# Mask rows spread over more slots, a new order on VectorE behind the encoder's attention, and a layer norm applied on ScalarE for three groups

## The chip, the cores and the metric

One core of one Trainium2 chip runs the whole program in one launch. The metric is device time in microseconds (us), of the slowest core where there are several; here there is one. Five engines with queues of their own take part: TensorE (PE), VectorE (DVE), ScalarE (ACT), GpSimd (POOL) and SyncE (SP), which here only issues DMAs. They wait for one another by semaphores written out by hand.

## The reference

The input x has shape 8 x 512 x 128. Two blocks follow each other, each as x + layernorm(block(layernorm(x))):

```python
# block 1: attention of all 4096 tokens to 512 shared keys, 16 heads of 8
q = relu(x @ Wq.T + bq); k = relu(keys @ Wk.T + bk); v = relu(values @ Wv.T + bv)
a = softmax(q k.T / sqrt(8)) v            # per head
out1 = transpose(a).reshape(x.shape) + x
# block 2: an encoder layer. Attention runs over the 8 batch rows, 4 heads of 32
y1 = ln1(x + mha(x))                      # "the norm behind the encoder's attention"
# top-1 routing to 8 experts with a capacity of 512 tokens; linear experts
gates = softmax(y1 @ wg); idx = argmax(gates)
y2 = ln2(y1 + gate * ((y1 @ w1[idx] + b1[idx]) @ w2[idx] + b2[idx], 0 if over capacity))
```

## The kernel before

**First part (to about 377 us).** The first attention is cut into 32 slots (`kappa` 0 to 31): half of the batch rows for two heads each. In a slot, PE computes the scores of 8 items by rows, VectorE takes their maxima out of PSUM (`reduce_rows`, eight per slot), GpSimd splits the maxima into three bf16 parts (`split_max`), PE turns them, ScalarE copies them (`max_turned`), and SP loads them by two DMAs as shift rows into the stack of the next slot (`load_shift`). PE then computes the scores by columns (`score_columns`, L1587), ScalarE takes the exponentials, and PE multiplies with v (`multiply_v`). SP's queue in a slot is, in this order: six DMAs of the stack three slots ahead (`load_stack`, L1294), in every fourth slot two of the keys (`load_keys`, L1299), the two shift rows (L1305), four stores of the attended rows (L1320). In slots 2 to 5, `load_c` (L1314) adds four DMAs each, sixteen in all, which spread the bf16 parts of the experts' combined bias over rows of `c_rows`. GpSimd copies these rows twice into `c_stack` in its slot 6, and writes the mask rows into it by two `affine_select` in slot 7 and two in slot 8 (L1494). The experts at the end need `c_stack`.

While the slots of one group of heads run, GpSimd finishes the group before: `pool_group` with `pool_divide` (the attended rows by their softmax sums), residual and two layer norms. The last group (g = 3) has no slots behind it, so that its part falls into the back end: `pool_divide` on GpSimd, the norms (called LAST1 and LAST2 here) on VectorE. LAST2 makes the encoder's input of group 3, announced by the semaphore `s_n2l`.

**Back end (from about 378 us).** The tokens are in four groups of 1024 (g = 0 to 3, eight tiles of 128 x 128). The encoder's attention takes each group in two halves, q = 0 to 7. The order on each engine is written out. For a half: PE `scores2(q)` (L623, L629), VectorE `compact(q)` (a maximum over PSUM, L944, then two small steps to L949), ScalarE `softmax_exp(q)` (L815), VectorE `normalise(q)` (L954 to L958), GpSimd `spread(q)` (L516, four instructions of 128 x 512), PE `spread_turned(q)` (L660), ScalarE two copies `copy_turned` (L820), PE `attend(q)` (L669), ScalarE `copy_attended(q)` (L826). For a group: PE `turn_tokens` and `project` (L608, L613), ScalarE's copies of them (L791, L797, L802), then PE `project_out(g)` (L677), VectorE `residual(g)` (L965), and the norm ln1: statistics and five small instructions (`norm_smalls`, L259 to L265), ScalarE's square root (`root`, L303), VectorE's `norm_invert` (L269, L271), and `norm_apply`, eight tensor_scalar of 128 x 128 (L280). GpSimd's `affine1(g)` (L527, four instructions) follows, and PE turns the result (`turn_y1`). VectorE then routes the group (`choose(g)`, L983 to L992) and selects among the experts (`select`, L1008), PE computing them tile by tile (L651, L653).

Exponential and square root lie in different tables of ScalarE; between them stands an ACT_TABLE_LOAD. A load stands right in front of its instruction and doesn't wait for what the instruction waits for.

Of the kernel before, what the change touches and what calls it, by code (L numbers as in the profile page):

```python
# [5 lines left out]
D = 128  # L6
B = 8
S = 512
G = S // P
NH, DH = 16, 8  # L10
NH2, HD2 = 4, 32
E, FF = 8, 512
E2 = E // 2
# [3 lines left out]
QB = 4  # L17
# [5 lines left out]
PARTS = 3  # L23
# [8 lines left out]
QPG = 2  # L32
# [20 lines left out]
def build(nc, x, keys, values, wq, bq, wk, bk, wv, bv, win, bin_, wout, bout,  # L53
# [8 lines left out]
    with ExitStack() as ctx:  # L62
# [3 lines left out]
        def sem(name):  # L66
            return ctx.enter_context(nc.semaphore(name))
# [9 lines left out]
        X = sb("X", [P, G, B, D])  # L77
# [34 lines left out]
        def view(space, lo, dims, dt=F32, parts=P):  # L112
# [6 lines left out]
            if len(dims) == 1:  # L119
# [99 lines left out]
             "logits_ready", "logits_copied", "expert_masks_ready", "gate_exp_done", "tokens_counted", "weights_ready"))  # L219
        (s_xp, s_sel, s_wa, s_i4, s_n4, s_i5, s_n5, s_y2, s_y2l, s_am, s_aq, s_asd, s_af1, s_sum2, s_out) = (sem(n) for n in  # L220
            ("experts_done", "expert_selected", "weighed_by_act", "norm4_scale_ready",
             "norm4_done", "norm5_scale_ready", "norm5_done", "output_ready", "last_output_ready", "act_means", "act_squares", "act_deviation_ready", "second_affine_done", "third_sum_ready", "output_stored"))
# [8 lines left out]
        def norm_variance(dve, ch, src, st6, small):  # L231

            for b in range(B):
                ins = dve.bn_stats(st6[:, b, :], src(b))  # L234
            ch.done(ins)
            ch.wait()
            norm_smalls(dve, ch, st6, small)

# [50 lines left out]
        def tiles(t, g):  # L289
            return lambda b: t[:, g, b, :]  # L290
# [115 lines left out]
        def pool_divide(pool, ch, g):  # L406

            pool.wait_ge(s_al, 64 * (g + 1))
            pool.wait_ge(s_rb, 64 * (g + 1))
            ch.done(pool.tensor_tensor(A[:, g], A[:, g], INV, MUL))  # L410
            ch.wait()
            pool.tensor_tensor(A[:, g], A[:, g], XN[:, g], ADD).then_inc(s_r1, 1)

# [373 lines left out]
        def back_end_act(act):  # L787
# [35 lines left out]
            def copy_attended(q):  # L823
# [4 lines left out]
                               ACT.Identity, bias=bias_col[:, 5:6]).then_inc(s_ot, 1)  # L828

            copy_tokens(1)  # L830
            softmax_exp(0)
# [15 lines left out]
            copy_attended(2)  # L847
            root(act, LAST2, smallo)
            copy_turned(3, 0, 4)
            copy_turned(3, 1, 6)  # L850
            softmax_exp(4)
            copy_attended(3)
            copy_y1(0, 6)
# [5 lines left out]
            copy_turned(4, 1, 6)  # L859
            copy_attended(4)  # L860
            softmax_exp(6)
            copy_logits(0)
# [8 lines left out]
            root(act, LN1[2])  # L871
            copy_attended(6)
            copy_logits(1)
            copy_turned(7, 0, 4)
# [65 lines left out]
        def back_end_dve(dve, ch):  # L940
# [27 lines left out]
            def variance1(g):  # L968
                dve.wait_ge(s_res, g + 1)
                norm_variance(dve, ch, tiles(A, g), st6, small)  # L970

            def apply1(g):
                norm_invert(dve, ch, LN1[g], small)
                norm_apply(dve, tiles(A, g), tiles(A, g), small).then_inc(s_n3, 1)

# [36 lines left out]
            compact(0)  # L1012
            normalise(0)
            dve_invert(dve, last)
            for q in range(1, 2 * QPG):
                compact(q)
                normalise(q)
            residual(0)
            dve.wait_ge(s_r1, G)
            norm_variance(dve, ch, tiles(A, last), st6o, smallo)  # L1020
            variance1(0)
            norm_invert(dve, ch, LAST1, smallo)
# [4 lines left out]
            ch.wait()  # L1027
            norm_variance(dve, ch, tiles(X, last), st6o, smallo)
            compact(4)
            norm_invert(dve, ch, LAST2, smallo)  # L1030
            norm_apply(dve, tiles(X, last), tiles(A, last), smallo).then_inc(s_n2l, 1)
            normalise(4)
            compact(5)
# [22 lines left out]
            residual(g)  # L1056
            dve.wait_ge(s_res, G)
            norm_variance(dve, ch, tiles(A, g), st6, small)
            select(5)
# [192 lines left out]
        def _(sp):  # L1252
# [54 lines left out]

            def load_c(k):

                sp.wait_ge(s_csplit, 1)  # L1310
                sp.wait_ge(s_cz, 1)
                c_k = c_rows[32 * k:32 * k + PARTS, :].rearrange("q (r j d) -> q r j d", r=2, d=D)
                for j in range(E2):
                    sp.dma_start(c_k[:, :, j, :], c_parts[32 * j:32 * j + 1]).then_inc(s_cl, 16)  # L1314
# [54 lines left out]
            def slot(kappa):  # L1369
# [12 lines left out]
                if kappa:  # L1382
                    sp.wait_ge(s_pve, kappa)
                    store_attended(kappa - 1)

            for kappa in range(NQ):
                g, c = kappa // 8, kappa % 8
                slot(kappa)
                if c == 1 and g:
                    load_denominators(g - 1)  # L1390
                if c == 2 and g:
                    load_attended(g - 1)
                    store_inverses(g - 1)
# [13 lines left out]
        def _(pool):  # L1407
# [61 lines left out]
            def build(kappa):  # L1469

                if kappa == 1:
                    pool.wait_ge(s_qp, B)
                    pool.memset(c_rows, 0.0).then_inc(s_cz, 1)
                if kappa == 5:
                    pool.wait_ge(s_wu, E)
                    pool.memset(others, 0.0).then_inc(s_oz, 1)
                if kappa == 2:
                    pool.wait_ge(s_const, 6)
                    for h in range(NH2):
                        ch.done(pool.affine_select(out=own_row[:], in_=own_row[:], compare_op=ALU.not_equal, fill=1.0,  # L1480
                                                   base=-HD2 * h, pattern=[[0, B], [-1, 16]], channel_multiplier=1))
                        ch.wait()
                    pool.tensor_scalar(other_row[:], own_row[:], -1.0, BIG, ADD, MUL).then_inc(s_rm, 1)
                if kappa == 6:
                    pool.wait_ge(s_cl, 16 * E2 * QB)
                    for v in range(2):
                        ch.done(pool.tensor_copy(c_stack[:, v, :].rearrange("p (d e) -> p e d", e=E),
                                                 c_rows.rearrange("p (e d) -> p e d", d=D)))
                    ch.wait()
                if kappa in (7, 8):  # L1490
                    c_v = c_stack[:].rearrange("p v (d e) -> p v d e", e=E)
                    for k in (2 * (kappa - 7), 2 * (kappa - 7) + 1):
                        pool.wait_ge(s_cb, k)
                        pool.affine_select(out=c_v, in_=c_v, compare_op=ALU.not_equal, fill=-BIG, base=-32 * k - MASK_ROW,  # L1494
                                           pattern=[[-E, 2], [0, D], [-1, E]], channel_multiplier=1).then_inc(s_cb, 1)
# [426 lines left out]
```

## Time and profile before

| | us |
|---|---|
| runs | 583.43, 583.67, 587.01: median 583.67 |
| the profiled execution | 585.64, of which the span of instructions 583.9 |
| busy: PE / DVE / ACT / POOL | 491.2 / 509.8 / 410.3 / 224.8 |
| mean granted TensorE clock | 0.946 of full speed |

All times below are those of the profiled execution, counted from the start of its span. In a timeline row stand start, duration, engine, line, operation, the written and read tiles with partitions x elements, how many instructions were merged, and in square brackets how long the engine had been idle before and what released it. The program's names are those of buffers: `space` stands for views of several large ones. A row merged from several instructions gives the time from the start of the first to the end of the last.

### The profile page before, as it was taken

To read this page: it belongs to the slowest core of one execution; us is meant where nothing else is said; L and a number is where in the kernel's file an instruction comes from. 1 tells how busy PE (TensorE), PEld (TensorE's weight loads), DVE (VectorE), ACT (ScalarE), POOL (GpSimd) and SP (SyncE) were. 2 spreads that over 40 slices of the span, in tenths; PEclk is the share of its full clock that TensorE was granted. 3 is DMA by queue.
4 is the path that set the end of the run, shared out by engine and by line. 5 is a ranking of instruction groups with operands and counts; after the bars stand their busy time and mean duration, and the time that the engine had idled before them with its cause. 6 is when DMAs were issued, how large, how long until landed. Compare 5 with 4: busy or idle time off the path is not lost.

```text
span 583.9 us, 10824 instructions
## 1 busy us (share of the span) xinstructions
PE 491.2 (84%) x3955; PEld 202.6 (35%) x3955; DVE 509.8 (87%) x821; ACT 410.3 (70%) x837; POOL 224.8 (38%) x345
## 2 busy tenths in 40 slices
PE   1887799989999999999999999887578898987900
PEld 1545122222222222222222222365457564433300
DVE  4979899969999999999999995369988759899986
ACT  1743499969999999999999998644446321144963
POOL 8000212029801766726676344868366330000000
PEclk9979599979999999999999999999988999999965
DMA  9945011111113111132111310020000000000112
GB/s 237 299 152 146 28 29 33 29 31 34 33 42 100 44 35 31 43 91 57 33 28 41 79 50 13 11 83 1 1 2 1 1 1 0 2 0 0 36 36 72
DMA packets 31796, 28.99 MB, mean 50 GB/s; under 512 B 6256, under 2 KB 23800, under 8 KB 31744
## 3 DMA queue, kind: packets, MB, share of 16 engines
q1 hardware_dynamic: 29712, 27.33, 16.8%
q10 hardware_dynamic: 2032, 0.98, 0.7%
q8 instruction: 31, 0.51, 0.4%
q14 instruction: 21, 0.17, 0.1%
HBM read 19.23 MB, written 8.65 MB: 48 GB/s over the span
## 4 chain that ended last, share of the span: by engine, by line
PE 48%; DVE 40%; ACT 7%; issue 3%; DMA 1%; SPq 0%; DVEq 0%; ACTq 0%
PE ps L1598 16%; DVE row_max L1845 16%; PE ps L1587 9%; PE ps L1560 8%; DVE space L1008 4%; PE ps L653 2%; DVE space L944 2%; ACT space L1767 2%; ACT space L897 2%; DVE st L234 1%; PE ps L608 1%; PE ps L660 1%; PE ps L343 1%; DVE space L280 1%; DVE XN L280 1%
## 5 line engine op out<-in xcount | busy, mean ns | idle before, releaser
L1845 DVE TENSOR_REDUCE row_max<-ps 128x2 f32<-128x1024 f32 x256 | 293.6, 1218 | 10.8 <-PE ps L1560 8.1
L1767 ACT ACTIVATE space<-ps 128x512 f32<-128x512 f32 x512 | 269.4, 598 | 13.7 <-PE ps L1587 10.5
L1598 PE MATMUL ps<-space 128*32 128x512 f32 (+1 forms) x1504 | 151.6, 475 | 0.4
L1560 PE MATMUL ps<-space 48*128 48x512 bf16 x512 | 132.8, 395 | 12.0 <-DVE row_max L1845 10.1
L1587 PE MATMUL ps<-space 51*128 51x512 bf16 x512 | 135.2, 388 | 1.9 <-DMA space<-max_turned 1.9
L1438 POOL CAST max_parts<-row_max 128x16 bf16<-128x16 f32 x32 | 6.3, 196 | 186.8 <-DVE row_max L1845 186.8
L1587 PEld LDWEIGHTS ps<-space 51*128 51x128 bf16 x512 | 41.2, 94 | 73.4 <-ACT space L1767 51.1
L653 PE MATMUL ps<-W,space 128*128 128x512 f32 x128 | 65.4, 592 | 0.0
L1560 PEld LDWEIGHTS ps<-space 48*128 48x128 bf16 x512 | 26.3, 94 | 72.9 <-DVE row_max L1845 37.4
L1598 PEld LDWEIGHTS ps<-space 128*32 128x32 f32 x1504 | 29.8, 108 | 62.7 <-issue 35.5
L1008 DVE TENSOR_REDUCE space<-ps 128x128 f32<-128x1024 f32 x32 | 38.6, 1218 | 9.0 <-PE ps L653 8.8
L516 POOL TENSOR_TENSOR space<-PC,same_row 128x512 f32<-128x512 f32 x32 | 33.0, 1062 | 18.9 <-DVE PC L958 11.0
L651 PE MATMUL ps<-c_stack,w1T 128*128 128x512 bf16 x64 | 24.4, 381 | 9.3 <-DVE space L1008 9.3
L653 PEld LDWEIGHTS ps<-W,space 128*128 128x128 f32 x128 | 24.4, 191 | 16.1 <-issue 14.4
L944 DVE TENSOR_REDUCE space<-ps 128x128 f32<-128x2048 f32 x8 | 18.2, 2278 | 6.6 <-PE ps L629 6.6
L527 POOL TENSOR_TENSOR space<-space,rows 128x512 f32<-128x512 f32 x12 | 15.0, 1268 | 18.9 <-DVE space L280 18.7
L303 ACT ACT_TABLE_LOAD x5 | 6.4, 1283 | 22.0 <-DVE small L265 22.0
L820 ACT COPY space<-ps 128x1024 f32<-128x1024 f32 x16 | 15.6, 1012 | 8.9 <-PE ps L660 8.9
L660 PE MATMUL ps<-ident,space 128*128 128x128 f32 x128 | 16.3, 281 | 5.0 <-issue 3.0
L1774 ACT COPY attended<-ps 128x512 f32<-128x512 f32 x32 | 18.7, 586 | 2.0 <-PE ps L1598 2.0
L425 POOL TENSOR_TENSOR XN<-XN 128x256 f32<-128x256 f32 (+4 forms) x40 | 15.8, 394 | 3.1
L660 PEld LDWEIGHTS ps<-ident,space 128*128 128x128 f32 x128 | 14.3, 143 | 7.0 <-issue 4.1
(245 smaller groups left out, 648.8 us busy)
## 6 DMA issues: line engine op xcount, KB each, us to landing
space<-q_parts_dram SPq DMA_DIRECT2D x64, 48.0 KB
attended_dram<-attended SPq DMA_DIRECT2D x128, 18.0 KB
X<-in_L_attn_queries SPq DMA_DIRECT2D x8, 256.0 KB, 7.5
space<-in_L_ffn_w SPq DMA_DIRECT2D x2, 1024.0 KB, 6.0
space<-q_parts_dram SPq DMA_DIRECT2D x64, 32.0 KB
space<-attended_dram SPq DMA_DIRECT2D x16, 128.0 KB, 2.9
space<-inverses_dram SPq DMA_DIRECT2D x16, 128.0 KB
out<-space SPq DMA_DIRECT2D x4, 512.0 KB, 3.2
```

The lines of the kernel that those rows point to most:

```text
L516: pool.tensor_tensor(EX[:, half, 4 * h:4 * h + 4, :].rearrange("p t (m n) -> p t m n", n=16), PC[:, q, 4 * h:4 * h + 4, :].rearrange("p t ...
L651: pe.matmul(ps[:, bank + half, :], others[:, g, b // 2, :], c_stack[:, b % 2, cols], start=True, stop=False)
L653: mm = pe.matmul(ps[:, bank + half, :], YT[:, g, b, :], W[:].rearrange("p d e -> p (d e)")[:, cols], start=False, stop=True)
L660: mm = pe.transpose(ps[:, bank + k // 4, (k % 4) * P:(k % 4 + 1) * P], EX[:, q % QPG, 8 * pair + k, :], ident[:])
L944: dve.tensor_reduce(SC[:, q].rearrange("p a m -> p (a m)"), ps[:, 0:4, :].rearrange("p a (t n) -> p (a t) n", n=16), AX.X, MAX).then_inc(s ...
L1008: dve.tensor_reduce(YT[:, k // B, k % B, :], ps[:, bank:bank + 2, :].rearrange("p a (d e) -> p (a d) e", e=E), AX.X, MAX).then_inc(s_sel, 1)
L1560: mm = pe.matmul(ring(n)[:, a, :], q_stack[rows_a, kappa % 4, item * P:item * P + P], k_rows[rows_a, kappa // 4 % 2, :], start=True, stop= ...
L1587: pe.matmul(ps[:, col_bank(v), :], k_rows[rows_a, kappa // 4 % 2, tc * P:(tc + 1) * P], q_stack[rows_a, kappa % 4, b * S:(b + 1) * S], sta ...
L1598: mm = pe.matmul(ps[32 * m:32 * m + 32, PV, cols], v_heads[:, tc, PAIR * (kappa // 4) + m % PAIR, :], probs[(TC * kappa + tc) % 3][:, m, c ...
L1767: act.activation(probs[(TC * kappa + tc) % 3][:, m, :], ps[:, col_bank(v), :], ACT.Exp, scale=1.0 / math.sqrt(DH)).then_inc(s_pr, 1)
L1774: act.copy(attended[:, kappa % 2, :], ps[:, PV, :]).then_inc(s_pve, 1)
L1845: dve.tensor_reduce(row_max[:, par].rearrange("p (a c) -> p a c", a=PAIR)[:, :, item], ring(n), AX.X, MAX).then_inc(s_free, 1)
```

## The change

`load_c` issues three DMAs in each of slots 2, 3, 4, 6, 7 and one in slot 8, where it issued four in each of slots 2 to 5. GpSimd's two copies into `c_stack` move from slot 6 to slots 9 and 10 (one each), its two pairs of mask rows from slots 7 and 8 to slots 11 and 19. The last group's `pool_divide` works on four pieces of two tiles.

In the back end VectorE takes `compact(1)` ahead of the last group's reciprocal, both statistics of LAST1 and ln1 of group 0 ahead of their small steps, and `compact(4)` and `normalise(4)` ahead of LAST2's inverse and apply. For groups 0 to 2 `norm_apply` of ln1 leaves VectorE: it announces the scale (`s_i1`), and ScalarE applies it by eight activations in a new `apply1(g)`, which stands behind `copy_attended` of half 2, 4 and 6. ScalarE's root for LAST2 moves behind `softmax_exp(4)`.

```diff
         def pool_divide(pool, ch, g):
...
-            ch.done(pool.tensor_tensor(A[:, g], A[:, g], INV, MUL))
-            ch.wait()
-            pool.tensor_tensor(A[:, g], A[:, g], XN[:, g], ADD).then_inc(s_r1, 1)
+            parts = [slice(0, B)] if g < G - 1 else [slice(lo, lo + 2) for lo in range(0, B, 2)]
+            for part in parts:
+                ch.done(pool.tensor_tensor(A[:, g, part], A[:, g, part], INV[:, part], MUL))
+            ch.wait()
+            for part in parts:
+                ins = pool.tensor_tensor(A[:, g, part], A[:, g, part], XN[:, g, part], ADD)
+            ins.then_inc(s_r1, 1)
...
+            def apply1(g):
+                act.wait_ge(s_i1, g + 1)
+                for b in range(B):
+                    ins = act.activation(A[:, g, b, :], A[:, g, b, :], ACT.Identity, scale=small[:, 3, b:b + 1],
+                                         bias=small[:, 4, b:b + 1])
+                ins.then_inc(s_n3, 1)
...
             copy_attended(2)
-            root(act, LAST2, smallo)
+            apply1(0)
             copy_turned(3, 0, 4)
             copy_turned(3, 1, 6)
             softmax_exp(4)
+            root(act, LAST2, smallo)
             copy_attended(3)
...
             copy_attended(4)
+            apply1(1)
             softmax_exp(6)
             copy_logits(0)
...
             copy_attended(6)
+            apply1(2)
             copy_logits(1)
...
             def variance1(g):
                 dve.wait_ge(s_res, g + 1)
+                dve.wait_ge(s_n3, g)
                 norm_variance(dve, ch, tiles(A, g), st6, small)
 
             def apply1(g):
-                norm_invert(dve, ch, LN1[g], small)
-                norm_apply(dve, tiles(A, g), tiles(A, g), small).then_inc(s_n3, 1)
+                norm_invert(dve, ch, LN1[g], small, s_i1)
...
             compact(0)
             normalise(0)
+            compact(1)
             dve_invert(dve, last)
-            for q in range(1, 2 * QPG):
+            normalise(1)
+            for q in range(2, 2 * QPG):
                 compact(q)
                 normalise(q)
             residual(0)
             dve.wait_ge(s_r1, G)
-            norm_variance(dve, ch, tiles(A, last), st6o, smallo)
-            variance1(0)
+            dve.wait_ge(s_res, 1)
+            norm_statistics(dve, tiles(A, last), st6o)
+            ch.done(norm_statistics(dve, tiles(A, 0), st6))
+            ch.wait()
+            norm_smalls(dve, ch, st6o, smallo)
+            norm_smalls(dve, ch, st6, small)
             norm_invert(dve, ch, LAST1, smallo)
             ch.done(norm_apply(dve, tiles(A, last), tiles(A, last), smallo))
             ch.wait()
             ch.done(dve.tensor_tensor(X[:, last], X[:, last], A[:, last], ADD))
             apply1(0)
             ch.wait()
-            norm_variance(dve, ch, tiles(X, last), st6o, smallo)
+            ch.done(norm_statistics(dve, tiles(X, last), st6o))
             compact(4)
+            ch.wait()
+            norm_smalls(dve, ch, st6o, smallo)
+            normalise(4)
             norm_invert(dve, ch, LAST2, smallo)
             norm_apply(dve, tiles(X, last), tiles(A, last), smallo).then_inc(s_n2l, 1)
-            normalise(4)
             compact(5)
             residual(1)
             normalise(5)
...
-            def load_c(k):
+            def load_c(lo, hi):
...
-                for j in range(E2):
+                for i in range(lo, hi):
+                    k, j = i // E2, i % E2
...
                     sp.dma_start(c_k[:, :, j, :], c_parts[32 * j:32 * j + 1]).then_inc(s_cl, 16)
...
+            C_SLOTS = (2, 3, 4, 6, 7, 8)
...
-                if 2 <= kappa < 2 + QB:
-                    load_c(kappa - 2)
+                if kappa in C_SLOTS:
+                    first = 3 * C_SLOTS.index(kappa)
+                    load_c(first, min(first + 3, E2 * QB))
...
-                if kappa == 6:
+                if kappa in (9, 10):
+                    v = kappa - 9
                     pool.wait_ge(s_cl, 16 * E2 * QB)
-                    for v in range(2):
-                        ch.done(pool.tensor_copy(c_stack[:, v, :].rearrange("p (d e) -> p e d", e=E),
-                                                 c_rows.rearrange("p (e d) -> p e d", d=D)))
+                    ch.done(pool.tensor_copy(c_stack[:, v, :].rearrange("p (d e) -> p e d", e=E),
+                                             c_rows.rearrange("p (e d) -> p e d", d=D)))
                     ch.wait()
-                if kappa in (7, 8):
+                if kappa in (11, 19):
                     c_v = c_stack[:].rearrange("p v (d e) -> p v d e", e=E)
-                    for k in (2 * (kappa - 7), 2 * (kappa - 7) + 1):
+                    for k in (0, 1) if kappa == 11 else (2, 3):
```

The last group's own ln1 stays on VectorE and only gains a wait for the third `apply1`.

## Rows read from the trace of the kernel before

**Rows 1.** Timeline of VectorE, slots 5 and 6 and those around them.

```profile
127.96 1.23 DVE L1845 TENSOR_REDUCE row_max<-ps 128x2 f32<-128x1024 f32 x1 [2.88 <-PE ps L1560]
130.86 2.44 DVE L1845 TENSOR_REDUCE row_max<-ps 128x2 f32<-128x1024 f32 x2 [1.68 <-PE ps L1560]
133.79 41.69 DVE L1845 TENSOR_REDUCE row_max<-ps 128x2 f32<-128x1024 f32 x36 [0.49 <-PE ps L1560]
```

**Rows 2.** Timeline of SP's DMA queue, slots 2, 5 and 7.

```profile
94.45 2.98 SPq L1314 DMA_DIRECT2D space<-c_parts  x4
...
121.38 1.55 SPq L1299 DMA_DIRECT2D space<-k_rows_dram  x2
122.97 1.51 SPq L1305 DMA_DIRECT2D space<-max_turned  x2
...
137.75 3.78 SPq L1294 DMA_DIRECT2D space<-q_parts_dram  x6
142.88 1.49 SPq L1305 DMA_DIRECT2D space<-max_turned  x2
144.42 1.51 SPq L1320 DMA_DIRECT2D attended_dram<-attended  x4
```

**Rows 3.** Timeline of PE in slot 5.

```profile
124.96 0.39 PE L1587 MATMUL ps<-space 51*128 51x512 bf16 x1 [1.49 <-DMA space<-max_turned]
```

**Rows 4.** Timeline of POOL, slot 7.

```profile
141.81 7.75 POOL L1494 TENSOR_SCALAR_AFFINE_SELECT c_stack<-c_stack 128x2048 bf16<-128x2048 bf16 x2
```

**Rows 5.** Timeline of ScalarE around the places of the new applies.

```profile
416.35 0.69 ACT L826 ACTIVATE space<-ps,bias_col 128x512 f32<-128x512 f32 x1 [1.22 <-PE ps L669]
422.10 0.30 ACT L303 ACTIVATE smallo<-smallo,eps 128x8 f32<-128x8 f32 x1 [5.07 <-DVE smallo L265]
...
424.23 1.28 ACT L815 ACT_TABLE_LOAD   x1
...
445.20 0.69 ACT L826 ACTIVATE space<-ps,bias_col 128x512 f32<-128x512 f32 x1 [1.22 <-PE ps L669]
...
447.81 0.31 ACT L815 ACTIVATE PC<-space 128x128 f32<-128x128 f32 x1 [0.62 <-DVE space L949]
448.02 0.19 ACT L811 COPY logits<-ps 128x64 f32<-128x64 f32 x1
```

**Rows 6.** The chain that ended last: an apply by ScalarE in a later norm.

```profile
534.69 3.19 ACT space L897 x8
```

**Rows 7.** Timeline of VectorE in the back end.

```profile
404.76 1.64 DVE L234 BATCH_NORM_STATS2 st6o<-space 128x6 f32<-128x128 f32 x8
...
425.27 2.14 DVE L280 TENSOR_SCALAR space<-X,smallo 128x128 f32<-128x128 f32 x8
...
433.06 1.23 DVE L965 TENSOR_TENSOR space<-ps,XN 128x1024 f32<-128x1024 f32 x1 [1.47 <-PE ps L677]
...
444.20 2.29 DVE L944 TENSOR_REDUCE space<-ps 128x128 f32<-128x2048 f32 x1 [1.73 <-PE ps L629]
...
450.35 0.95 DVE L987 TENSOR_SCALAR space<-space 128x64 f32<-128x64 f32 x1
...
473.19 0.20 DVE L987 TENSOR_SCALAR space<-space 128x64 f32<-128x64 f32 x1
...
478.64 1.23 DVE L1008 TENSOR_REDUCE space<-ps 128x128 f32<-128x1024 f32 x1 [2.10 <-PE ps L653]
```

**Rows 8.** Timeline of POOL in the back end.

```profile
416.99 5.05 POOL L527 TENSOR_TENSOR space<-space,rows 128x512 f32<-128x512 f32 x4 [9.08 <-DVE space L280]
...
449.18 4.10 POOL L516 TENSOR_TENSOR space<-PC,same_row 128x512 f32<-128x512 f32 x4 [1.56 <-issue]
```

**Rows 9.** Timeline of PE in the back end.

```profile
424.33 0.61 PE L623 MATMUL ps<-other_row,own_row 32*128 32x512 bf16 x4 [5.27 <-DVE space L944]
...
435.06 3.70 PE L608 MATMUL ps<-space,wT 128*128 128x512 f32 x8 [1.16 <-ACT space L791]
```

**Rows 10.** Busy time by stretch (PE, PEld, DVE, ACT, POOL), granted PE clock, DMA share, GB/s.

```profile
424.00:431.00 7.00, 5.51 (x77) 4.48 (x77) 6.72 (x19) 3.57 (x6) 2.65 (x3) 0.64 0.00 0
```

More of the change, by code:

```diff
@@ L219, in build @@
              "logits_ready", "logits_copied", "expert_masks_ready", "gate_exp_done", "tokens_counted", "weights_ready"))
-        (s_xp, s_sel, s_wa, s_i4, s_n4, s_i5, s_n5, s_y2, s_y2l, s_am, s_aq, s_asd, s_af1, s_sum2, s_out) = (sem(n) for n in
-            ("experts_done", "expert_selected", "weighed_by_act", "norm4_scale_ready",
+        (s_xp, s_sel, s_wa, s_i1, s_i4, s_n4, s_i5, s_n5, s_y2, s_y2l, s_am, s_aq, s_asd, s_af1, s_sum2, s_out) = (sem(n) for n in
+            ("experts_done", "expert_selected", "weighed_by_act", "norm1_scale_ready", "norm4_scale_ready",
              "norm4_done", "norm5_scale_ready", "norm5_done", "output_ready", "last_output_ready", "act_means", "act_squares", "act_deviation_ready", "second_affine_done", "third_sum_ready", "output_stored"))
@@ L231, in norm_variance, with norm_statistics @@
         def norm_variance(dve, ch, src, st6, small):
+            ch.done(norm_statistics(dve, src, st6))
+            ch.wait()
+            norm_smalls(dve, ch, st6, small)
+        def norm_statistics(dve, src, st6):
             for b in range(B):
                 ins = dve.bn_stats(st6[:, b, :], src(b))
-            ch.done(ins)
-            ch.wait()
-            norm_smalls(dve, ch, st6, small)
+            return ins
         def st64(g):
@@ L1019, in back_end_dve @@
             dve.wait_ge(s_r1, G)
-            norm_variance(dve, ch, tiles(A, last), st6o, smallo)
-            variance1(0)
+            dve.wait_ge(s_res, 1)
[3 more added lines that the diff above has]
+            norm_smalls(dve, ch, st6o, smallo)
+            norm_smalls(dve, ch, st6, small)
             norm_invert(dve, ch, LAST1, smallo)
@@ L1057, in back_end_dve @@
             dve.wait_ge(s_res, G)
+            dve.wait_ge(s_n3, g)
             norm_variance(dve, ch, tiles(A, g), st6, small)
@@ L1306, in load_shift @@
                                  max_turned[turned, kappa % 2, :]).then_inc(s_shift[a], 16)
-            def load_c(k):
+            def load_c(lo, hi):
                 sp.wait_ge(s_csplit, 1)
                 sp.wait_ge(s_cz, 1)
-                c_k = c_rows[32 * k:32 * k + PARTS, :].rearrange("q (r j d) -> q r j d", r=2, d=D)
-                for j in range(E2):
+                for i in range(lo, hi):
+                    k, j = i // E2, i % E2
+                    c_k = c_rows[32 * k:32 * k + PARTS, :].rearrange("q (r j d) -> q r j d", r=2, d=D)
                     sp.dma_start(c_k[:, :, j, :], c_parts[32 * j:32 * j + 1]).then_inc(s_cl, 16)
```

## The prediction

> **What bounds the kernel now.** I read the page first: PE and VectorE are both busy for some 85% of the span, so the mean tells nothing, and each stage has to be read by itself. I took the timeline of VectorE for the first part. A slot is eight maxima over PSUM, and they run back to back: 36 in 41.69 us, 1.158 each, so a slot takes 9.26 us [rows 1]. That is VectorE's pace, and only in slots 5 and 6 does it break: idle times of 2.88, 1.68 and 0.49 us, 5.05 in all, put down to PE. PE in its turn waited there 1.49 us for the shift rows [rows 3], which SP issued late. So SP's queue binds two slots of the first part.
>
> In the back end I read the timelines of all five engines beside each other, since every step of a half waits for the one before it on another engine. Two places bear on the change. ScalarE stands 5.07 us at LAST2's root [rows 5], holding up the copies behind it, and PE then resumes after 5.27 us of idle time [rows 9]. And behind `copy_attended(4)` ScalarE has 0.62 us to spare after its table load before `softmax_exp(6)` [rows 5]: VectorE, GpSimd and PE all go on from that exponential.
>
> **Mask rows.** In a plain slot SP's issues take 3.78 + 1.49 + 1.51 = 6.78 us of 9.26 [rows 2]; 2.48 are free. Four DMAs of `load_c` take 2.98 and don't fit: three slots in a row fall behind, and in slot 5 the keys' 1.55 come on top. Three DMAs take 2.24 and fit. What remains is slot 5: the keys stand ahead of the shift, and the stack starts late behind slot 4's three. On time the shift would be at 142.88 - 2 x 9.26 - 5.05 = 119.3. Of the 2.48 free us 142.88 - 137.75 - 3.78 = 1.35 lie between stack and shift and 1.13 ahead of the stack; 2.24 of `load_c` make the stack 1.1 late and leave 0.2 ahead of the shift, and the keys add 1.55, so it goes out near 120.7. PE would have taken it without waiting if issued by 122.97 - 1.49 = 121.5. That leaves 0.8 us. I take the whole 5.05 as gained; the lower bound is half of it, if slot 5 still stalls. SP isn't late in slot 9, since slot 8 gets one DMA only. GpSimd's mask rows take 7.75 us for two [rows 4]; with that in slot 7 VectorE ran its 36 maxima without a gap [rows 1], so slots 11 and 19, where no group work stands, hold it as well. The copies, one to a slot, are shorter. `c_stack` isn't needed before the experts. All this costs nothing while GpSimd's slot lasts under 9.26; without that cover it would cost the excess.
>
> **The reorder up to group 0.** LAST1's small steps now stand behind eight more statistics, 1.64 us [rows 7], and ScalarE's copies of group 2's projections queue behind LAST1's root. Against this VectorE comes earlier to that place, since `compact(1)` no longer waits behind the reciprocal and the waits for exponentials are filled; I estimate 0 to 2.3 us. So `copy_attended(2)`, which ends at 416.35 + 0.69 = 417.04 [rows 5], moves by +1.6 to -0.7; I take +0.5, 417.5. `pool_divide` in four pieces has the same elements and six more instructions; it starts later, because the reciprocal does, but is wanted only behind `residual(0)`. I price it at 0 (bounds 0 and +0.5: GpSimd's next `spread` is put off).
>
> **Apply on ScalarE, group 0.** Eight activations of this shape took 3.19 us in a later norm [rows 6]. From 417.5 ScalarE does apply 3.19, two copies 424.23 - 422.40 = 1.83, table 1.28, exponential 0.31, table 1.28, root 0.30 [rows 5]: 425.7. Two table loads are new, because exponential and root of LAST2 have changed places. VectorE has `compact(4)` done long before and waits. GpSimd's `affine1(0)`, 5.05 us [rows 8], now runs from 420.7 to 425.8, and `normalise(4)`, a product of two SBUF operands, ends with it. The inverse takes 0.4, and LAST2's apply can start at 426.4 instead of 425.27.
>
> Here is the step I am least sure of. `normalise(4)` now goes first and releases `spread(2,0)`, so the apply's eight tensor_scalar run beside four GpSimd instructions, 4.10 us. No row shows these eight beside a GpSimd tensor_tensor. The nearest: a tensor_scalar of `choose(0)` took 0.95 us beside `spread`, and 0.20 without [rows 7, 8]. The bounds are 2.14 (no hindrance), so 428.5 for `s_n2l`, and one instruction let through per GpSimd instruction: 426.05 + 4.10, then five of 0.27, 431.5. It was 427.4. I take 431.5, by the nearer row.
>
> From there VectorE does `compact(5)` (444.20 to 447.81 for its like, of which some 0.65 was hindrance: 2.95) and `residual(1)` 1.2; PE follows 0.25 later: `project(3)` at 435.9, against 435.06 [rows 9], +0.85. Before, VectorE waited 1.47 us for PE ahead of that residual [rows 7]; this wait is gone, and what is late is VectorE itself.
>
> **Apply on ScalarE, groups 1 and 2.** VectorE saves 2.14 each, but behind group 1 it waited 1.73 us for PE anyway [rows 7]: worth nothing. ScalarE pays: `copy_attended(4)` ended at 445.89; with +1.0 (the 0.85, and small steps of group 1 a little more hindered) 446.9. Then apply 3.19, table 1.28, exponential 0.31: 451.7, against 448.12 [rows 5], +3.6. Behind it are queued `copy_logits(0)`, for which PE waits, and VectorE's `normalise(6)`, `choose(0)` and `compact(7)`, which was busy without a break before. These meet `affine1(1)` (1.26 per instruction) where they met `spread` (1.03): +0.4. For group 2 the logits come 2 us later and `choose(1)` runs beside `affine1(2)`: up to 4 x 0.75 = 3.0, of which 2.10 vanish in VectorE's wait ahead of a select [rows 7]; +0.6 (bounds 0 and +1.0). From there on VectorE runs nearly without a gap, so the rest moves along.
>
> **Sum.** -5.05 + 1.0 + 2.6 + 0.4 + 0.6 = -0.45 us. The profiled execution would be 585.64 - 0.45 = 585.2; it lies 1.97 above the median of the runs, so against the median 583.67 I predict 583.2.
>
> **Rivals.**
> *The apply isn't hindered.* `s_n2l` comes at 428.5, `project(3)` at 432.9, 2.15 early; `softmax_exp(6)` is still 0.55 late, since apply and table load stand in front of it. Back end +1.55, net -3.5: 580.2. Against it stands the 0.95 row; for it, that those instructions waited for each other by semaphores and these eight don't. On this the Trainium skill, "SBUF — State Buffer", section "Who interferes with whom", says that the pair of ports that VectorE and GpSimd share is an exclusive lock which the first to start holds for its whole instruction. By that rule, VectorE getting in first would block GpSimd instead, and the time would be this rival's; the 0.95 row shows GpSimd first.
> *Slower: TensorE's clock.* In the forecast PE idles some 3 us ahead of `project(3)`, where it idled 1.16. After 5.27 us of idle time the stretch behind had a granted clock of 0.64, a mixture of 1.2 and 2.4 GHz [rows 9, 10]. If `project(3)` (3.70 us) falls to the lower level, the first half of it takes 1.85 more, and the rest some 0.5 that ScalarE's root doesn't hide: net +1.9, 585.6. It decides as soon as the granted clock in that stretch is below 1.
> *The mask rows don't do what they should.* Slot 5 still stalls: half gained gives 585.7, nothing gained 588.3. The 0.8 us of room speak against it.
> *All goes well:* the reorder gains its 0.7, nothing hinders, and group 2 costs nothing: 578.4 or less.
>
> **How the numbers follow.** Forecast 0.44, apply not hindered 0.24, clock 0.15, mask rows 0.10, better than all that 0.07. The range 578.5 to 587.0 leaves out the last and the worst parts of the second and third rival, some 0.15. A change under 1% (5.8 us) can hardly be told from none in this kernel, by the spread of the three runs. Under 577.8 lies most of the best case and a little of errors I don't see: 0.10; over 589.5 0.05; 0.85 between.
>
> **What would show it.** VectorE's idle times of slots 5 and 6 are gone, and the slots' maxima follow each other at 9.26 us; SP's shift of slot 5 goes out behind the keys without PE waiting. ScalarE shows five more microseconds between `copy_attended(2)` and LAST2's root, two more table loads, and `softmax_exp(6)` directly behind one. LAST2's eight tensor_scalar take about 5 us together, or 2.14 if the first rival holds. The prediction is wrong if the applies start at other times than given (a wait for `s_i1` on ScalarE would do it), or if VectorE has idle time behind group 3's residual that takes the delay back.

## The result, and the profile after

The changed kernel is slower: 589.91 us (median of 13 runs, 586.38 to 592.62) against 584.08 us for the kernel before beside it (13 runs, 581.80 to 587.38); ratio 1.0088, 95% interval 1.0067 to 1.011. The prediction was 583.2, range 578.5 to 587.0, with 0.85 on a change of less than 1%: the ratio lies within that 1%, the time outside the range. The profiled execution took 588.79 us with a span of 587.1, 3.2 above the span of before. That is less than the 5.1 us of the ratio, because before's profiled execution lies 1.6 us above the median of its kernel and that of the changed kernel 1.1 below; the traces hold only part of the difference.

**The first part did what the forecast said.** The timeline of VectorE in the changed kernel (start, duration, engine, line, operation, count, idle time before), which answers to [rows 1]:

```profile
72.65 97.25 DVE L1875 TENSOR_REDUCE row_max<-ps 128x2 f32<-128x1024 f32 x84 [1.71 <-PE ps L1590]
```

84 maxima in 97.25 us without a gap, 1.158 each: the three idle times of before are gone. SP's queue around slot 5, which answers to [rows 2]:

```profile
112.71 2.25 SPq L1342 DMA_DIRECT2D space<-c_parts  x3
115.01 3.78 SPq L1321 DMA_DIRECT2D space<-q_parts_dram  x6
118.83 0.77 SPq L1326 DMA_DIRECT2D space<-k_rows_dram  x2
119.65 1.51 SPq L1332 DMA_DIRECT2D space<-max_turned  x2
```

The shift of slot 5 went out at 119.65, against 120.7 forecast and 121.5 needed, mostly because the keys took 0.77 us here and not 1.55. The back end's `compact(0)` starts at 374.85 instead of 380.20: 5.35 us gained.

**The back end gave it all back, and 3.2 us more.** So I counted its steps from the start of `compact(0)` in either trace:

| step, us since `compact(0)` | before | after | moved | forecast |
|---|---|---|---|---|
| LAST1's root, ScalarE | 28.17 | 29.77 | +1.6 | |
| `copy_attended(2)` | 36.15 | 38.88 | +2.7 | +0.5 |
| LAST2's root | 41.90 | 47.37 | +5.5 | +3.3 |
| end of LAST2's apply (`s_n2l`) | 47.21 | 53.52 | +6.3 | +4.1 |
| `project(3)` | 54.86 | 57.73 | +2.9 | +0.85 |
| `softmax_exp(6)` | 67.61 | 73.50 | +5.9 | +3.6 |
| `compact(7)` | 73.09 | 79.36 | +6.3 | +4.0 |
| `residual(2)` | 79.46 | 87.36 | +7.9 | +4.0 |
| `residual(3)` | 100.58 | 109.04 | +8.5 | +4.6 |
| end of the span | 203.70 | 212.25 | +8.55 | +4.6 |

The forecast errs in two steps: 2.2 us by `copy_attended(2)`, and 1.6 between `compact(7)` and `residual(2)`. Everything between keeps its distance from the forecast.

*The first step* begins behind LAST1's statistics. VectorE's timeline of the changed kernel there (before: [rows 7]):

```profile
399.94 1.63 DVE L240 BATCH_NORM_STATS2 st<-space 128x6 f32<-128x128 f32 x8
401.60 0.55 DVE L263 TENSOR_TENSOR smallo<-st6o 128x8 f32<-128x8 f32 x1
402.07 1.09 DVE L264 TENSOR_TENSOR smallo<-st6o 128x8 f32<-128x8 f32 x1
403.09 1.09 DVE L265 TENSOR_TENSOR smallo<-st6o 128x8 f32<-128x8 f32 x1
404.21 0.17 DVE L267 SCALAR_TENSOR_TENSOR smallo<-smallo 128x8 f32<-128x8 f32 x1
```

GpSimd's timeline beside it:

```profile
390.24 2.84 POOL L416 TENSOR_TENSOR space<-space 128x256 f32<-128x256 f32 x4 [2.05 <-DMA space<-inverses_dram]
393.15 2.82 POOL L419 TENSOR_TENSOR space<-space,XN 128x256 f32<-128x256 f32 x4
395.94 8.21 POOL L524 TENSOR_TENSOR space<-PC,same_row 128x512 f32<-128x512 f32 x8
```

And GpSimd's timeline of the kernel before, with the same divide and the later of the two `spread`:

```profile
394.17 2.37 POOL L410 TENSOR_TENSOR space<-space 128x1024 f32<-128x1024 f32 x1
396.61 2.35 POOL L412 TENSOR_TENSOR space<-space,XN 128x1024 f32<-128x1024 f32 x1
...
403.79 4.13 POOL L516 TENSOR_TENSOR space<-PC,same_row 128x512 f32<-128x512 f32 x4 [0.44 <-DVE PC L958]
```

The divide waits 2.05 us for the inverses, since the reciprocal comes later now, and in its four pieces it takes 5.73 us (390.24 to 395.97) where it took 4.79. So two `spread` run back to back until 404.15; counted from `compact(0)` that is 1.6 later than before. LAST1's small steps on tiles of 128 x 8, 0.17 us each when alone (404.21), take up to 1.09 beside them. Before, too, they began beside `spread`, but it ended 1.5 us after they started (407.92); now it ends 2.6 after. The root is 1.6 late, of which 0.5 are the eight statistics moved ahead, less what VectorE gained, as forecast, and 1.1 the small steps. As an estimate from these rows, the divide in one piece would have let `spread` end 0.9 earlier; no run tried it. PE then has stood idle for 3.75 us (1.07 before), and the 32 matmuls of projection V and `spread_turned` take 2.53 and 3.13 us where they took 2.05 and 1.95; 1.1 of that reaches `copy_attended(2)`.

*The second step* is `project_out(2)`. PE's timeline of the kernel before, at the projection V, at `spread_turned` and at `project_out(2)`:

```profile
409.73 2.05 PE L613 MATMUL ps<-wT,space 128*128 128x128 f32 x16 [1.07 <-ACT space L797]
412.10 1.95 PE L660 MATMUL ps<-ident,space 128*128 128x128 f32 x16 [0.32 <-issue]
...
457.57 2.05 PE L677 MATMUL ps<-wT,space 128*128 128x128 f32 x16 [2.44 <-ACT space L807]
```

PE's timeline of the changed kernel, from the first step on (the rows of `project(3)` and ahead of it answer to [rows 9]):

```profile
405.97 2.53 PE L621 MATMUL ps<-wT,space 128*128 128x128 f32 x16 [3.75 <-ACT space L805]
408.30 3.13 PE L668 MATMUL ps<-ident,space 128*128 128x128 f32 x16
...
425.81 3.78 PE L685 MATMUL ps<-wT,space 128*128 128x128 f32 x16 [1.16 <-ACT space L815]
...
432.58 3.70 PE L616 MATMUL ps<-space,wT 128*128 128x512 f32 x8 [1.28 <-ACT space L799]
...
458.49 3.68 PE L685 MATMUL ps<-wT,space 128*128 128x128 f32 x16 [3.02 <-ACT space L815]
```

The windows of the changed kernel (length, busy time of PE, PEld, DVE, ACT and POOL with counts, granted clock, DMA share, GB/s; [rows 10] is the third of before):

```profile
404.00:419.00 15.00, 10.87 (x152) 9.92 (x152) 10.03 (x37) 10.81 (x18) 1.58 (x3) 0.89 0.01 1
419.00:424.00 5.00, 2.40 (x38) 2.14 (x39) 2.94 (x5) 4.04 (x6) 4.64 (x5) 0.70 0.00 0
424.00:431.00 7.00, 5.84 (x28) 5.33 (x26) 6.91 (x11) 2.36 (x3) 5.39 (x4) 0.50 0.00 0
...
445.00:454.00 9.00, 5.23 (x77) 4.87 (x80) 5.32 (x9) 5.75 (x11) 6.81 (x6) 0.81 0.00 0
454.00:462.00 8.00, 4.98 (x41) 4.54 (x34) 4.69 (x11) 1.96 (x4) 5.75 (x7) 0.79 0.00 0
```

`project_out(2)`, 16 matmuls, takes 3.68 us after 3.02 idle; before, it took 2.05. VectorE waits for it with `residual(2)`: the 1.6 us. `project_out(1)` ran wholly at the lower level (granted 0.50 in its window), `project(3)` at the upper one (granted 0.99 from 431 to 445).

*As forecast* are the steps of ScalarE from `copy_attended(2)` to LAST2's root. Its timeline in the changed kernel, which answers to [rows 5]:

```profile
413.73 0.69 ACT L834 ACTIVATE space<-ps,bias_col 128x512 f32<-128x512 f32 x1 [1.25 <-PE ps L677]
414.31 3.18 ACT L841 ACTIVATE space<-space,small 128x128 f32<-128x128 f32 x8
417.39 1.90 ACT L828 COPY space<-ps 128x1024 f32<-128x1024 f32 x2
419.31 1.28 ACT L823 ACT_TABLE_LOAD   x1
420.60 0.31 ACT L823 ACTIVATE PC<-space 128x128 f32<-128x128 f32 x1
420.93 1.28 ACT L307 ACT_TABLE_LOAD   x1
422.22 0.30 ACT L307 ACTIVATE smallo<-smallo,eps 128x8 f32<-128x8 f32 x1
```

So is LAST2's apply. VectorE's timeline, which answers to [rows 7], and then GpSimd's beside it ([rows 8]):

```profile
424.02 4.35 DVE L284 TENSOR_SCALAR space<-X,smallo 128x128 f32<-128x128 f32 x8
```

```profile
422.90 4.11 POOL L524 TENSOR_TENSOR space<-PC,same_row 128x512 f32<-128x512 f32 x4 [0.28 <-issue]
```

The apply has `spread` beside it until 427.01. After that 1.36 us remain, which is five instructions at 0.27 (2.14 / 8); so three got through in 2.99 us, about one per GpSimd instruction of 1.03.

### The profile page after: what moved, and what is told of

Its sections match the earlier page's. It is cut to its first block, busy times and chain, and to the rows that moved or that the text cites. A ratio compares the mean times of both kernels' runs of the same rounds, so it can differ in the third digit from the quotient of the medians.

```text
span 587.1 us, 10839 instructions
## 1 busy us (share of the span) xinstructions
PE 492.0 (84%) x3955; PEld 207.2 (35%) x3955; DVE 505.8 (86%) x797; ACT 421.6 (72%) x863; POOL 225.8 (38%) x351
## 4 chain that ended last, share of the span: by engine, by line
PE 48%; DVE 39%; ACT 7%; issue 2%; DMA 1%; ACTq 1%; DVEq 0%
DVE row_max L1875 18%; PE ps L1628 16%; PE ps L1617 9%; PE ps L1590 8%; DVE space L1026 4%; PE ps L661 2%; ACT space L915 2%; PE ps L668 2%; DVE space L962 2%; DMA w_in<-in_L_ffn_out_proj_w 1%; PE ps L616 1%; DVE space L284 1%; PE ps L347 1%; ACT space L841 1%; PE ps L621 1%
## 5 line engine op out<-in xcount | busy, mean ns | idle before, releaser
L1628 PE MATMUL ps<-space 128*32 128x512 f32 (+1 forms) x1504 | 150.0, 471 | 0.4
L1617 PE MATMUL ps<-space 51*128 51x512 bf16 x512 | 133.6, 384 | 0.0
L668 PE MATMUL ps<-ident,space 128*128 128x128 f32 x128 | 18.6, 304 | 6.9 <-issue 4.7
L668 PEld LDWEIGHTS ps<-ident,space 128*128 128x128 f32 x128 | 16.7, 160 | 9.0 <-issue 5.7
```

Source lines behind the costliest of these rows:

```text
L668: mm = pe.transpose(ps[:, bank + k // 4, (k % 4) * P:(k % 4 + 1) * P], EX[:, q % QPG, 8 * pair + k, :], ident[:])
L1617: pe.matmul(ps[:, col_bank(v), :], k_rows[rows_a, kappa // 4 % 2, tc * P:(tc + 1) * P], q_stack[rows_a, kappa % 4, b * S:(b + 1) * S], sta ...
L1628: mm = pe.matmul(ps[32 * m:32 * m + 32, PV, cols], v_heads[:, tc, PAIR * (kappa // 4) + m % PAIR, :], probs[(TC * kappa + tc) % 3][:, m, c ...
```

## The experiments

A profile's first part differs from execution to execution: `compact(0)` started at 372.86 to 376.07 in ten kernels with the new mask rows. So beside each ratio (to the kernel before, run beside it on the same chip) the table gives the back end of the profiled execution, from `compact(0)` to the end of the span.

| kernel | median us | ratio, 95% interval | back end us |
|---|---|---|---|
| before | 584.1 to 585.5 | 1 | 203.7 |
| changed | 589.91 | 1.0088 [1.0067, 1.011] | 212.25 |
| mask_rows_only | 580.07 | 0.9912 [0.988, 0.9943] | 204.6 |
| back_end_only | 594.27 | 1.0149 [1.0119, 1.018] | 212.45 |
| reciprocal_early | 587.90 | 1.0045 [1.0026, 1.0063] | 211.3 |
| applies_on_vector | 584.46 | 0.9986 [0.9963, 1.0009] | 207.3 |
| group1_on_vector | 587.44 | 1.0037 [1.001, 1.0064] | 210.8 |
| apply_before_normalise | 588.67 | 1.0074 [1.0043, 1.0104] | 211.9 |
| changed_pe_filled | 587.28 | 1.0037 [1.0017, 1.0056] | 210.6 |
| mask_rows_compact4 | 579.61 | 0.9916 [0.9886, 0.9947] | 203.0 |
| mask_rows_filled | 583.99 | 0.9978 [0.9961, 0.9995] | 205.5 |
| compact4_filled | 581.02 | 0.9929 [0.9909, 0.9948] | 203.9 |

**The two halves of the change, each alone.** `mask_rows_only` is the kernel before with this part of the change:

```diff
-                if 2 <= kappa < 2 + QB:
-                    load_c(kappa - 2)
+                if kappa in C_SLOTS:                     # (2, 3, 4, 6, 7, 8)
+                    first = 3 * C_SLOTS.index(kappa)
+                    load_c(first, min(first + 3, E2 * QB))
...
-                if kappa == 6:
+                if kappa in (9, 10):
...
-                if kappa in (7, 8):
+                if kappa in (11, 19):
```

> The kernel before with the mask rows alone spread over more slots (SP's and GpSimd's part of the change). If the first part did what the two traces show, the back end starts 5.3 us earlier and nothing gives it back: ratio to before 0.991, VectorE without idle time in slots 5 and 6. If the rival holds, that an earlier start of the back end costs it time of its own (by the place of its idle times against TensorE's clock), less than 3 us remain: 0.995 or more.

Measured 0.9912, 5.1 us gained. Its maxima on VectorE's timeline run as in the changed kernel:

```profile
71.12 97.28 DVE L1848 TENSOR_REDUCE row_max<-ps 128x2 f32<-128x1024 f32 x84 [1.29 <-PE ps L1563]
```

`back_end_only` is the changed kernel with these lines as before.

> The changed kernel with the mask rows as before. If the loss is the back end's own, it shows in full: 8.5 us between its start and its end as in the two traces, ratio 1.015. If the loss comes from the two parts together, under 1.010.

Measured 1.0149. The halves add up within the noise: 0.9912 x 1.0149 = 1.0060, uncertain by some 0.0044, against 1.0088 for both. The mask rows are worth what was forecast for them; all the rest of the change costs some 8.7 us. The back end of `back_end_only` took as long as that of the changed kernel, but lost its time at other places: there the projection V took 3.78 us after 4.25 of idle time, and `project_out(2)` 2.05 after 2.32. So the 1.6 us at `project_out(2)` are those of the changed kernel's profiled execution; the same order can lose more at the first step and nothing there.

**The late reciprocal.**

```diff
             compact(0)
             normalise(0)
-            compact(1)
             dve_invert(dve, last)
+            compact(1)
             normalise(1)
```

> The changed kernel with the last group's reciprocal ahead of compact(1), where it was. My theory: the late reciprocal makes the inverses land late, GpSimd's division and both spreads of group 1 follow 1.6 us later, and they hinder LAST1's small steps, behind which ScalarE's copies and PE's V projection wait; PE's idle time of 3.75 us there lowers its clock. Then LAST1's root comes 1.5 us earlier, copy_attended(2) 2 to 2.7 us, and the ratio falls from 1.009 to about 1.004. Rival: the eight statistics put ahead of those small steps are the delay; then less than 0.5 us change.

Measured 1.0045, as the number said, but not in the way that the theory said. GpSimd is through with `spread` at 403.35, and LAST1's small steps take 0.17 each. Yet the root comes only 0.56 us earlier counted from `compact(0)`, where 1.5 were expected, because VectorE itself got to the statistics 1.7 later. Of these, 1.0 come from other small steps that had met GpSimd instead (396.07 and 398.06 below; the same two took 0.35 and 0.77 in the changed kernel). VectorE's timeline of `reciprocal_early`:

```profile
396.07 1.00 DVE L967 TENSOR_TENSOR space<-space,mx 128x128 f32<-128x128 f32 x1
...
398.06 1.10 DVE L976 TENSOR_TENSOR PC<-PC,sm 128x128 f32<-128x128 f32 x1
...
403.62 0.17 DVE L263 TENSOR_TENSOR smallo<-st6o 128x8 f32<-128x8 f32 x1
```

PE's timeline of the same run:

```profile
405.75 2.05 PE L621 MATMUL ps<-wT,space 128*128 128x128 f32 x16 [1.64 <-ACT space L805]
...
431.14 5.20 PE L616 MATMUL ps<-space,wT 128*128 128x512 f32 x8 [2.42 <-ACT space L799]
```

What it did win is PE's clock at the projection V (2.05 us after 1.64 idle): `copy_attended(2)` is 1.76 earlier. Further on it lost part of that, by the very event of the slower rival in the prediction: `project(3)` took 5.20 us instead of 3.70. What is left is 0.9 us by the back end and 2.5 by the ratios, uncertain by some 1.7.

**The applies back on VectorE**, all three, and in another kernel group 1's alone.

```diff
# ScalarE
             copy_attended(2)
-            apply1(0)
... the same behind copy_attended(4) and copy_attended(6)
# VectorE, apply1(g), for g = 0 to 2
-                norm_invert(dve, ch, LN1[g], small, s_i1)
+                norm_invert(dve, ch, LN1[g], small)
+                norm_apply(dve, tiles(A, g), tiles(A, g), small).then_inc(s_n3, 1)
```

> The changed kernel with the three applies of ln1 back on VectorE, all else as changed. If the applies on ScalarE are the main loss, groups 0, 1 and 2 give back about 1, 2.5 and 0.6 us and what PE's clock loses behind them (1.6): 5 to 6 us, ratio 0.999. If the order of VectorE is the main loss, less than 2.5 us come back: 1.005 or more.

> The changed kernel with the apply of group 1 alone back on VectorE. By the prediction's step for group 1, softmax_exp(6) comes 2.5 us earlier and compact(7) 2.5 to 2.9: ratio 1.004. If VectorE's own apply (2.14 us) then delays compact(6), less than 1 us: 1.007.

Measured 0.9986 and 1.0037, as the numbers said. So moving the applies cost about 5 us of the back end (212.25 against 207.3), and the rest of the new order, with the divide in pieces and the two new table loads, 2.7 (207.3 against 204.6 for the mask rows alone); by the ratios 6.0 and 4.3. Group 1's apply by itself is worth 1.4 us by the back end, 3.0 by the ratios, uncertain by some 2. Its steps didn't move as expected: counted from `compact(0)`, `softmax_exp(6)` came 0.7 us earlier and `compact(7)` 1.1, not 2.5, for in that execution `project(3)` started 0.9 later and took 5.40 us instead of 3.70. With all three applies back, PE still idled 4.18 us ahead of the projection V, and later 3.06 ahead of `project(3)`, and both ran slow, as PE's timeline of `applies_on_vector` shows:

```profile
405.34 2.95 PE L621 MATMUL ps<-wT,space 128*128 128x128 f32 x16 [4.18 <-ACT space L805]
...
429.24 5.85 PE L616 MATMUL ps<-space,wT 128*128 128x512 f32 x8 [3.06 <-ACT space L799]
```

**LAST2's apply out of `spread`'s way.**

```diff
-            normalise(4)
             norm_invert(dve, ch, LAST2, smallo)
             norm_apply(dve, tiles(X, last), tiles(A, last), smallo).then_inc(s_n2l, 1)
+            normalise(4)
```

> The changed kernel with LAST2's inverse and apply ahead of normalise(4) again, so that no GpSimd spread runs beside the apply. The eight tensor_scalar then take 2.14 us instead of 4.35 and s_n2l comes some 3 us earlier. If that hindrance is on the path (as the prediction has it), project(3) starts 2 us earlier: ratio 1.005. Rival: project_out(1) on a slow PE (3.78 us) and turn_tokens(3) behind it end as late as exp(5), so that at most 0.5 us is won: 1.008.

Measured 1.0074, not to be told from the change. The eight instructions took 2.14 us, with GpSimd idle beside them, and were done 3.0 us earlier counted from `compact(0)`. VectorE's timeline of this run:

```profile
422.78 2.14 DVE L284 TENSOR_SCALAR space<-X,smallo 128x128 f32<-128x128 f32 x8
```

PE made little of it: `project_out(1)` still ran at the lower level, the turns behind it (428.28) came late, and `project(3)` started only 0.8 us earlier, as the rival in the expectation had it. Its timeline:

```profile
424.71 3.79 PE L685 MATMUL ps<-wT,space 128*128 128x128 f32 x16 [1.16 <-ACT space L815]
428.28 1.91 PE L599 MATMUL ps<-ident,space 128*128 128x128 f32 x8
431.36 3.70 PE L616 MATMUL ps<-space,wT 128*128 128x512 f32 x8 [1.16 <-ACT space L799]
```

**TensorE kept busy where it idles.**

```diff
+            def fill(bank, n):
+                for _ in range(n):
+                    pe.matmul(ps[:, bank, :], wT[:, 3, :], W[:].rearrange("p d e -> p (d e)")[:, 0:512], start=True, stop=True)
...
+                if g == 2:                       # ahead of projection V
+                    pe.wait_ge(s_msk, 4)
+                    fill(0, 3)
...                                               # around turn_y1(0): 2 and 1, bank 5
+                    pe.wait_ge(s_msk, 7)         # behind route(0)
+                    fill(0, 3)
...
+                    pe.wait_ge(s_msk, 8)         # ahead of project_out(2)
+                    fill(0, 2)
```

> The changed kernel with extra products on PE whose results nobody reads: 3 of 128 x 512 in the idle time ahead of group 2's V projection, 2 and 1 ahead of turn_y1(0) and project_out(1), 3 behind route(0), 2 ahead of project_out(2). They add work to PE and change nothing else. If the lower TensorE clock behind PE's idle times is what the sum left out, the granted clock stays near 1.0 there, project_out(2) takes 2.05 us instead of 3.7, the V projection and the turns behind it some 1.5 less: 3 us in all, ratio 1.003 to 1.004. If the slow PE is hidden behind other engines, or the added work costs what it saves, 1.008 or more.

Measured 1.0037: some 3 us come back without any of the program's own work being moved (uncertain by 1.7; 1.6 by the back end). The granted clock is 1.00 in three stretches where it was 0.89, 0.81 and 0.79, and `project_out(2)` takes 2.05 us. The windows of this run, then PE's timeline:

```profile
404.00:419.00 15.00, 10.96 (x179) 8.95 (x181) 10.29 (x37) 11.62 (x19) 2.79 (x3) 1.00 0.00 1
...
445.00:454.00 9.00, 6.73 (x90) 4.40 (x89) 5.32 (x9) 6.14 (x11) 7.01 (x7) 1.00 0.00 0
454.00:462.00 8.00, 6.32 (x40) 4.58 (x41) 6.08 (x14) 2.02 (x4) 5.75 (x7) 1.00 0.01 2
```

```profile
406.24 2.05 PE L628 MATMUL ps<-wT,space 128*128 128x128 f32 x16 [1.30 <-ACT space L819]
...
422.21 3.78 PE L611 MATMUL ps<-W,wT 128*128 128x512 f32 x4 [2.73 <-ACT space L848]
...
458.29 2.05 PE L692 MATMUL ps<-wT,space 128*128 128x128 f32 x16
```

The fill at 422.21 (two products, each recorded as two) missed: it came when PE had already idled 2.73 us, ran at the lower level itself, and held up `turn_y1(0)`. What the projection V had won was lost there: `project(3)` starts 58.3 us after `compact(0)`, against 57.7 without the fills.

**A better version?** `mask_rows_only` already beats both kernels. Three more tried to go below it. `mask_rows_compact4` adds to it, without ScalarE's applies, the change's idea of filling the 5 us of ScalarE:

```diff
# ScalarE
-            root(act, LAST2, smallo)
             copy_turned(3, 0, 4)
             copy_turned(3, 1, 6)
+            root(act, LAST2, smallo)
             softmax_exp(4)
# VectorE
-            norm_variance(dve, ch, tiles(X, last), st6o, smallo)
+            ch.done(norm_statistics(dve, tiles(X, last), st6o))
             compact(4)
+            ch.wait()
+            norm_smalls(dve, ch, st6o, smallo)
```

> The kernel before with the mask rows spread, compact(4) ahead of LAST2's small steps, and ScalarE's root for LAST2 behind the two copies of half 3 but ahead of softmax_exp(4) (so no new table loads); the applies stay on VectorE. ScalarE's wait of 5.07 us ahead of those copies should go, PE should turn to attend(3) some 4 us earlier and without 5 us of idle time, and project(3) start 3 to 4 us earlier: ratio 0.985. If VectorE's chain bounds that stretch anyway, 0.990 as with the mask rows alone.

Measured 0.9916, so no gain that the ratios can tell. By the profile `project(3)` came 2.6 us earlier than with the mask rows alone, though `project_out(1)` fell to the lower level (3.58 us); 1.0 was lost next to a `normalise(5)` that now met GpSimd, on VectorE's timeline:

```profile
426.07 1.63 DVE L964 TENSOR_TENSOR PC<-PC,sm 128x128 f32<-128x128 f32 x1
```

(0.66 with the mask rows alone). The back end is 1.6 us shorter in that one execution; the intervals are too wide for it. Then the same products on PE went into both kernels.

> The kernel before with the mask rows spread as in the change, nothing of the back end moved, and products on PE (128x512, resident tiles, results read by nobody) where it idles: three ahead of group 2's projection V, three around turn_y1(0), three behind route(0), two ahead of project_out(2). Theory that TensorE's clock costs time in the kernel with the mask rows alone too (its granted clock was 0.87 in 404:419, 0.69 in 419:424, 0.91 in 431:445, 0.88 in 445:454 and 0.86 in 454:462): most of these stretches go to 1.00, and some 2 to 3 us go as they did in the changed kernel: ratio 0.986 to 0.988 against the kernel before (mask rows alone: 0.991). Rival, the mask rows' kernel waits for VectorE in these stretches and not for PE: granted clock up, ratio 0.991 as without, or 0.992 to 0.993 if a fill gets in the way of the work behind it.

> The kernel of mask_rows_compact4 (mask rows spread, compact(4) ahead of LAST2's small steps, LAST2's root behind the copies of half 3) with the same products on PE where it idles. Theory that this order's gain of some 3 us at group 0 was lost to the clock (project_out(1) took 3.58 us at a granted clock of 0.66): project_out(1) takes 2.05, and the ratio is 0.984 to 0.986. Rival, the gain is lost to small steps beside GpSimd further on: 0.990 to 0.991 as without.

Measured 0.9978 and 0.9929: the gain that both theories expected isn't there. The first even lies above what its rival allowed (0.993) and clear of the same kernel without fills (0.9961 to 0.9995 against 0.988 to 0.9943), so there the fills cost something; the second can't be told from the kernel without them. The clock did rise (1.00 in 404 to 419, 0.98 to 1.00 from 424 on), but in `mask_rows_only` PE idles just 1.07 us ahead of the projection V and loses nothing there, so that the fill only pushed it back. PE's timeline of `mask_rows_filled`:

```profile
404.35 2.74 PE L603 MATMUL ps<-W,wT 128*128 128x512 f32 x6
406.93 1.95 PE L620 MATMUL ps<-wT,space 128*128 128x128 f32 x16
```

V starts 1.3 us later counted from `compact(0)`, `project(3)` 2.2. Both back ends are 0.9 us longer than without the fills. The ratio of `mask_rows_filled` lost more than that (3.9 us); in the profile another 1.9 lie in the first part, which the fills don't touch and which differs by up to 3.2 us among the ten kernels. Where those come from stays open.

## Why the prediction was wrong

- **Mask rows: right.** -5.05 forecast, -5.35 in the profile, 5.1 by the experiment.
- **The reorder up to group 0: the step that failed.** I took +0.5 (bounds -0.7 to +1.6); measured +2.7. The statistics' 1.64 less what VectorE gained came out at 0.5 as worked out. What the term left out: GpSimd's `spread` ends later and so stands longer beside LAST1's small steps (+1.1). The later divide in four pieces was priced at 0, with 0.5 as the bound for a `spread` put off, and I had not asked what VectorE does by then. The wait for the inverses was 2.05 us, and the pieces took 0.94 more for the same elements. `reciprocal_early` took that meeting away and won 0.56 at the root; no run put the divide back into one piece, so how the 1.1 is shared between the two isn't shown. And PE's longer idle time ahead of the projection V brought the lower clock (+1.1). By the experiments the new order without the applies costs 2.7 us of the back end.
- **TensorE's clock: the second failure.** The slower rival had the mechanism and looked at one place only. In the changed kernel `project(3)` kept its 3.70 us, with only 1.28 us of idle time ahead of it, since PE was busy with a slow `project_out(1)` until then. The clock cost 1.1 at the projection V and 1.6 at `project_out(2)`. Filling PE's idle time brought both back to 2.05 us, which shows that cause. The place isn't fixed: in `back_end_only` the projection V lost more and `project_out(2)` nothing. The rival's own place did occur in two variants (5.20 and 5.85 us for `project(3)`). The sum put that rival at 585.6 because it allowed one such event.
- **LAST2's apply is hindered: right.** 4.35 us, against 5 forecast and 2.14 for the first rival, by the mechanism taken: three in 2.99 us beside `spread`, five after it. By the rule of the Trainium skill that the rival cited ("SBUF — State Buffer", section "Who interferes with whom"), the first to start holds the ports. The trace agrees: `spread` started 1.1 us ahead of the apply, and GpSimd's four took their 4.11, as the `spread` of other halves did (4.10 to 4.15). So the case in which VectorE wins didn't occur. What it was worth is another matter: `apply_before_normalise` took the hindrance away and gained nothing that can be measured. The sum had put 3.0 us between the two cases at `project(3)`; the run shows 0.8, because the slow `project_out(1)` was next on the path.
- **Groups 1 and 2 on ScalarE: right in size.** Added from `project(3)` to `softmax_exp(6)` +3.0 against +2.75, to `compact(7)` +0.4 against +0.4, from `residual(2)` to `residual(3)` +0.6 against +0.6. These are steps of one trace; by experiment all three applies together cost about 5 us of the back end.
- **The range** allowed the clock once and the reorder 1.6 at most. The two misses, 2.2 and 1.6 us, together make 3.8 of the 3.95 between the back end's +8.55 and the forecast's +4.6. The medians differ by 5.8 us where -0.45 was forecast; the traces hold 3.15 of that, and the other 2.7 are the places of the two profiled executions among the runs of their kernels.

## What to carry to other kernels

When steps are moved, lay the new timelines of VectorE and GpSimd beside each other and look for the small steps that now fall beside a long GpSimd instruction: here each cost about 1 us instead of 0.17. Two edits of the order (`reciprocal_early`, `mask_rows_compact4`) moved such meetings, at least in part, to other steps, and the one that took a meeting away (`apply_before_normalise`) gained nothing, since another wait was next. Price the pieces when an instruction is cut up: GpSimd's divide of the same elements took 0.94 us more as eight instructions than as two. Give every stage in which PE will wait longer a term for its clock, at each such place and not at one, and fill PE's idle time only where the trace shows that matmuls on the path run slow. Measure the parts of a change each alone: one half of this one was worth 0.9%, the other cost 1.5%.

## What the runs showed of the hardware

The same 16 matmuls of `project_out(2)` took 2.05 us after 2.44 us of idle time (before) and after 2.32 (`back_end_only`), but 2.65 after 2.43, 2.85 after 2.40, 3.29 after 2.60, 3.42 after 2.66, 3.61 after 3.04 and 3.68 after 3.00 and 3.02 in other kernels. Those of `project_out(1)` took 2.05 after 2.67 in `applies_on_vector` and 3.78 after 1.16 in the changed kernel, so the last idle time alone doesn't decide. And VectorE's operations don't suffer alike beside GpSimd's tensor_tensor: reductions, statistics and reciprocals keep their 0.28, 1.64 and 0.25 us, while a product of two SBUF operands took 1.22 and 1.63 instead of 0.29, and eight tensor_scalar 4.35 instead of 2.14.
